# Identity transposes placed in TensorE's program order during the first batch of a two-layer decoder kernel

## What is computed

```python
x = _layernorm(x + _L0_attn_ref(x, ...))      # layer norm, 256->1024 projection, 4-tap convolution, selective scan over 16 states, gate, 512->256
x = _layernorm(x + _L0_xattn_ref(x, ctx_768, ...))   # cosine similarity of projected x and projected context
x = _layernorm(x + _L0_ffn_ref(x, ...))       # 4 low-rank experts, best 2, 256->1024->256
x = _layernorm(x + _L1_attn_ref(x, ...))      # 16 query heads, 4 key heads, rotary positions, low-rank additions to the weights
x = _layernorm(x + _L1_xattn_ref(x, ctx_768, ...))   # single-head attention over the context
x = _layernorm(x + _L1_ffn_ref(x, ...))       # gated recurrence over the 8 batches, c = f*c + i*g, then tanh(x wo + c_final uo + bo)
```

## Time and profile before

| | us |
|---|---|
| median of 3 executions | 1187.26 (1186.92 to 1191.86) |
| the profiled execution, its own time | 1190.96 |
| its span, first to last instruction | 1189.1 |
| TensorE busy (PE in the rows) | 1077.9, 91% of the span |
| VectorE busy (DVE) | 1007.3, 85% |
| ScalarE busy (ACT) | 763.1, 64% |
| GpSimd busy (POOL) | 210.1, 18% |
| mean granted TensorE clock, share of full speed | 0.945 |

### The profile page before, as it was taken

The page is one execution under the profiler, slowest core; times in us unless marked ns, Lnnn a source line. Parts: engine busy times, 40 slices in busy tenths (PEclk is TensorE's granted clock), DMA queues, the critical chain, the costliest instruction groups (busy, mean ns, idle before and its releaser), DMA issues. The chain is left out here.

```text
span 1189.1 us, 17415 instructions
## 1 busy us (share of the span) xinstructions
PE 1077.9 (91%) x6154; PEld 794.7 (67%) x6154; DVE 1007.3 (85%) x1690; ACT 763.1 (64%) x2010; POOL 210.1 (18%) x257
## 2 busy tenths in 40 slices
PE   5574869999999999999999999999999999999984
PEld 3353556665778677776786688767875877677763
DVE  3989899999999999999999999999999994334316
ACT  4525335677767876788667876877677656637533
POOL 0200010021221313130313141313211211010002
PEclk8666859999999999999999999999999999999997
DMA  5421211122333333342434143423342321000302
GB/s 220 152 101 50 71 43 36 46 63 64 84 76 103 72 82 71 63 112 59 94 63 114 28 115 71 119 38 72 89 122 37 79 54 32 1 1 10 128 13 71
DMA packets 41193, 86.70 MB, mean 73 GB/s; under 512 B 3737, under 2 KB 14970, under 8 KB 40466
## 3 DMA queue, kind: packets, MB, share of 16 engines
q1 hardware_dynamic: 27282, 60.42, 15.8%
q0 software_dynamic: 13824, 25.17, 12.2%
HBM read 54.38 MB, written 6.04 MB: 51 GB/s over the span
## 5 line engine op out<-in xcount | busy, mean ns | idle before, releaser
L561 ACT ACTIVATE scans<-dt,a_neg 128x255 f32<-128x255 f32 x512 | 224.1, 499 | 0.1
L632 POOL DMA_DIRECT2D scans<-scans x96 | 84.6, 882 | 422.1 <-DVE scans L606 421.7
L606 DVE TENSOR_TENSOR scans<-scans,BC 128x1024 f32<-128x1024 f32 x128 | 155.7, 1216 | 0.1
L598 DVE TENSOR_TENSOR_SCAN scans<-scans 128x1024 f32<-128x1024 f32 x64 | 146.0, 2281 | 2.7 <-ACT scans L561 2.7
L598 DVE TENSOR_TENSOR_SCAN scans<-scans,dBx_odd 128x1024 f32<-128x1024 f32 x64 | 146.0, 2282 | 2.6 <-ACT scans L561 1.8
L1392 ACT ACTIVATE ya<-bank,nmax 128x256 f32<-128x256 f32 x240 | 111.0, 474 | 41.2 <-issue 28.6
L532 PE MATMUL bank<-ident,scans 128*128 128x128 f32 x640 | 104.3, 302 | 31.2 <-DVE scans L606 30.9
L532 PEld LDWEIGHTS bank<-ident,scans 128*128 128x128 f32 x640 | 84.7, 156 | 53.8 <-DVE scans L606 34.4
L1459 DVE TENSOR_REDUCE nmax<-bank 128x2 f32<-128x512 f32 x128 | 84.6, 682 | 30.6 <-PE bank L1306 30.2
L558 ACT ACTIVATE scans<-neghalf 128x4 f32<-128x4 f32 x128 | 26.7, 208 | 90.1 <-PE bank L532 90.0
L1401 ACT ACTIVATE ya<-bank 128x512 f32<-128x512 f32 x120 | 68.6, 601 | 24.4 <-PE bank L1315 18.8
(11 more groups left out here) (273 smaller groups left out, 2327.3 us busy)
## 6 DMA issues: line engine op xcount, KB each, us to landing
BC<-xpj_scratch SPq DMA_DIRECT2D x31, 1024.0 KB, 5.8
scans<-scans POOLq DMA_DIRECT2D x96, 256.0 KB, 3.3
xin<-in_x SPq DMA_DIRECT2D x8, 256.0 KB, 3.0
conv<-in_x SPq DMA_DIRECT2D x8, 256.0 KB, 3.0
out<-scans SPq DMA_DIRECT2D x8, 256.0 KB, 2.1
kept_x<-x SPq DMA_DIRECT2D x7, 256.0 KB, 3.1
kept_w<-wa SPq DMA_DIRECT2D x7, 256.0 KB, 2.0
BC<-kept_w SPq DMA_DIRECT2D x1, 1792.0 KB, 9.2
```

What stands on the lines that cost most here:

```text
L561: ins = act.activation(step[:, j, 1:S], dt[b % 2][:, c, 1:S], ACT.Exp, scale=a_neg[:, c, n:n + 1])
L598: dve.tensor_tensor_scan(H, H, flat(dBx[u % 2]), 0.0, ALU.mult, ALU.add).then_inc(s["a_scan"], 1)
L606: dve.tensor_tensor(H, H, Ch, ALU.mult).then_inc(s["a_hC"], 1)
L632: pool.dma_start(flat(H[:, 0:2, :]), flat(H[:, 2:4, :]), accum_op=ALU.add).then_inc(SUM_OF[(NU * b + u) % 3], 16)
```

## The change

A new stage K for TensorE, and 87 letters K put into TensorE's list. A piece of K is four transposes of the 128x128 identity, into the four quarters of bank 7. It waits for nothing and signals nothing. Nothing reads what it writes. No letter of the old list moves, and the lists of the other engines stay as they are. 4 times 87 is 348 new matmul instructions and as many weight loads.

```diff
+N_IDLE = 87
...
 ORDER = {
     "pe": (
-        "FFFFFFFFFFSFSSSSSFFYWSFWYSSSFFSYSSFSSFYSSYWFSYGGGWGSSSFWWWYWSWYWYSSYWYSWSFWYFFWSWWWWWWSWWWWYWWFWWYFWWWWWSWWWWY"
...
+        "FFFFFFFFFFSKKFSSKKKKSKKKKKKKKSKKKKSKKFKKKKKKFYWSFWYSSKKKKKKKSKKKKKFFSYKKKSKKKKKKKKKKKKKSFSKKKKSKKKKFYSKKKSYWFS"
+        "YGGGWGKKKKSSSFKKWWWYKKWSWYWKKKKKYSSYKKWYSWKKKKKKKSFWYFFWSWWWWWWSWWWWYWWFWWYFWWWWWSWWWWYFYSFYSYYYYWYYYYFSYYYSYY"
...
+        def idle_pe(pe):
+            for _ in range(N_IDLE):
+                for t in range(4):
+                    pe.transpose(y2[:, t * P:(t + 1) * P], ident[:, :], ident[:, :])
+                yield
...
-                        "V": all_batches(lambda b: v_pe(pe, b))}, ORDER["pe"])
+                        "V": all_batches(lambda b: v_pe(pe, b)),
+                        "K": idle_pe(pe)}, ORDER["pe"])
```

More of the change, by code:

```diff
@@ L47 @@
     "pe": (
-        "FFFFFFFFFFSFSSSSSFFYWSFWYSSSFFSYSSFSSFYSSYWFSYGGGWGSSSFWWWYWSWYWYSSYWYSWSFWYFFWSWWWWWWSWWWWYWWFWWYFWWWWWSWWWWY"
-        "FYSFYSYYYYWYYYYFSYYYSYYFYYSYYYSSVVGGGYYGYFVVSFYYFWWWYWWSWVSYVYSYVVFWFYWYYWSYVYVWFSWWWYWVVWYSYWFWWYWWVSVWWFWWSW"
-        "WWWWYWWYWWVVVSSVVVVVVVYFWYYSWWYWYYWWYSWWYYWYYSYSWYYWSYWWYWWWWWWWYYSWYWWSVVGYWGYGGYVVSYYSSWYWVVWWSYYWYWWFVVFYYV"
-        "FVYSWWWYFYFYVWVWWWWYYWWSYWSWYFWWVVWWFSWWYWWWWWWWSWWVVVVVVVVVSVYSFWYYWWYWYYWWYSWWYYWYSWYYSWYSWYWYWWWYWWSWWYWSYW"
@@ L52 @@
[L52 to L56, removed]
@@ L57 @@
-        "VVSVWVYWWYSYYYWYYYWWYSWWYYWSYWYWYYWSWYWWWWWWWWYSYWWSYVGGWGGVYYWYWWWVVYYWYWWVVYYYVVWYYWYVVWYYWVYVWWWWYYWWVYVWWY"
-        "YWWVVWWVVWWVWWWWWWWWWVVVVVYWYYYYYYYYYYWWYYWYYWYWYWYWYVVYWYYWVVYYWWYWVYYWWWWYVYWYWYVVYYYWWWWYVVWVVYYYVVYVVVVVVV"
-        "WVVVWWWWWWWWWWWWWWWWWWWWWWWWWWWWWWW"
+        "FFFFFFFFFFSKKFSSKKKKSKKKKKKKKSKKKKSKKFKKKKKKFYWSFWYSSKKKKKKKSKKKKKFFSYKKKSKKKKKKKKKKKKKSFSKKKKSKKKKFYSKKKSYWFS"
+        "YGGGWGKKKKSSSFKKWWWYKKWSWYWKKKKKYSSYKKWYSWKKKKKKKSFWYFFWSWWWWWWSWWWWYWWFWWYFWWWWWSWWWWYFYSFYSYYYYWYYYYFSYYYSYY"
@@ new lines @@
+        "FYYSYYYSSVVGGGYYGYFVVSFYYFWWWYWWSWVSYVYSYVVFWFYWYYWSYVYVWFSWWWYWVVWYSYWFWWYWWVSVWWFWWSWWWWWYWWYWWVVVSSVVVVVVVY"
+        "FWYYSWWYWYYWWYSWWYYWYYSYSWYYWSYWWYWWWWWWWYYSWYWWSVVGYWGYGGYVVSYYSSWYWVVWWSYYWYWWFVVFYYVFVYSWWWYFYFYVWVWWWWYYWW"
+        "SYWSWYFWWVVWWFSWWYWWWWWWWSWWVVVVVVVVVSVYSFWYYWWYWYYWWYSWWYYWYSWYYSWYSWYWYWWWYWWSWWYWSYWVYFSVWWGYYGGYGVVSYYSSSV"
+        "YWVWWYYWYWWVFWVYSYFFYVVYWSYWYFFVVWWYYWWWYVWWVFWSYYWWFVVWWVSVWWVWWVWSWWWWWWWVWSVVVFSYWYYSWWYWYYYWWSYWYWYYWYWSSY"
+        "WWYWYWWWYSWWWWWSYYWVYSWWVGYGYGGYVVSSYSWFYWSWWYVVWYYWYVWVYSYYSVVFWYYWYFFWVVWYYSWWWWFWFWVYVWWYSYWWVVWWSVFWWVFWVW"
@@ new lines @@
+        "WWSWWWWWVVVVSVYFYWSYWWYWYYWWYSWWYYYSWYWYYSWWYWYWWYWSWWWWWYSYWSWWGYVGGVGYYSSSFWYVVWWYWYYSWWVWYVYSYVVFFFWYYWYVVS"
+        "YWYSVYWFFWWWWVYWWYSWWVYVWWFWYWYSVVVWWVWWWFWSWWWWWSVVVVVVSYFWYYYWYWYSYWYWWYYWWYSWYWYSYWWWYWWSWWWYWWSWWSYWGWYGGG"
+        "YSSWSFWVVWYWSYWYWWVVYYSYVVWWYWYSVYWVWWYWSWYWWYVVWSWYYWWYWWYVVWSYWWYWWWWVVYYWSWWWVVVVVSVVVSVWVYWWYSYYYWYYYWWYSW"
+        "WYYWSYWYWYYWSWYWWWWWWWWYSYWWSYVGGWGGVYYWYWWWVVYYWYWWVVYYYVVWYYWYVVWYYWVYVWWWWYYWWVYVWWYYWWVVWWVVWWVWWWWWWWWWVV"
+        "VVVYWYYYYYYYYYYWWYYWYYWYWYWYWYVVYWYYWVVYYWWYWVYYWWWWYVYWYWYVVYYYWWWWYVVWVVYYYVVYVVVVVVVWVVVWWWWWWWWWWWWWWWWWWW"
@@ L60 @@
+        "WWWWWWWWWWWW"
     ),
```

## The result

The changed kernel takes 1181.9 us (median of 7 executions, 1180.9 to 1184.1), the kernel before 1188.59 us (median of 7, 1186.92 to 1191.86). The ratio is 0.9936, with a 95% interval of 0.9923 to 0.995: faster by 0.64%, some 6.7 us by the medians. The forecast was 1174.8 us, so the direction was right and the size, 12.5 us, was nearly double the truth. The profiled execution took 1180.91 us, its span is 1179.1 us.

The account below looks back on a forecast made before the run. VectorE was taken to bound the kernel from 35 to 180 us, waiting 14.5 us on a TensorE slowed by its clock. Seven wait terms sum to 12.5 us, taken from the 1187.26 us median: 1174.8 us, range 1169 to 1186.

Parts of the forecast that it names:

- The bound: From 35 to 180 us VectorE bounds; its 14.5 us of waits for TensorE are the most to gain, handed on unchanged.
- The pieces at no cost: The 87 pieces, at most 47 us at full clock, fit TensorE's 51.3 us of idle time and cost nothing.
- Transposes as activity: Float32 transposes against the identity count as activity and raise TensorE's clock, against the Trainium skill's rule.
- L1583: VectorE's 3.2 us wait: the projection and low-rank product ahead shrink to half, 2.0 us gained.
- The two waits at L448: VectorE's waits of 2.6 and 0.8 us: combined weight and projections ahead shrink, 2.1 and 0.8 us gained.
- L1612: VectorE's 1.4 us wait: half of the 2.07 + 1.87 us ahead exceeds it, so all is gained.
- L613: VectorE's 3.7 us wait: work ahead shrinks by 2.7 us, 4.1 with earlier gains, so all is gained.
- L865: VectorE's 2.2 us wait: L532 and the logits shrink by 1.7 us, work ahead by about 1; all gained.
- L913: VectorE's 0.6 us wait: chain already at full clock, TensorE somewhat earlier; half taken, 0.3 us gained.
- I take the clock to stay at 1.00 from the second block on: TensorE's clock, mean 0.68 from 35 to 180 us, would be near 1.00; the 12.5 us sum assumes it.
- the first rival: Half the gain: waits grow as work shrinks, the clock falls again in one or two; 1181 us, chance 0.18.
- The rival on the other side: Slower: pieces run at 1.2 GHz and overrun their waits by 25 to 35 us; +13 us, 1200 us, chance 0.10.

Follow-up runs that it names:

- f3: The changed kernel with twice the pieces in each block (174 in place of 87); 1188.9 us, ratio 0.9985 to the kernel before.
- e2: The changed kernel with each piece two plain 128-row identity products in place of four transposes; 1183.0 us, ratio 0.9935 to the kernel before.
- e1: The changed kernel with each piece two one-row products in place of four transposes; 1204.5 us, ratio 1.0109 to the kernel before.
- e3: The changed kernel with 33 more pieces (120) where TensorE still idled; 1175.9 us, ratio 0.9888 to the kernel before.
- f1: The changed kernel with 33 more pieces where TensorE idled, 22 at the start and 2 more (144); 1173.8 us, ratio 0.9857 to the kernel before.
- f4: The changed kernel with only its first six blocks (26 pieces, up to 60 us); 1186.4 us, ratio 0.9975 to the kernel before.

## Why the prediction was right in direction and double in size

- **The bound** held. VectorE's idle time in the first batch was what could be won, and what was won there arrived at the end. (The digits of rows 1 go down to 5, not to 6; nothing rests on it.)
- **The pieces at no cost** held, with one small exception. The 7 pieces ahead of unit 6 of batch 1 ran mostly at half clock (6.05 us from 164.35), and L534 behind them started at 170.24, 1.6 us after VectorE's product was there (168.64). Behind it L913's wait became 0.1 us longer. f3 shows what it costs when the cover is gone.
- **Transposes as activity** held: the clock rose from 0.68 to 0.91 with them, and e2 shows products of the same size doing no more.
- **The terms, one by one.** L1583: 2.0 forecast, 3.2 to 1.4 is 1.8 measured. The two waits at L448: 2.9 forecast, 3.4 to 0.4 is 3.0. These stand ahead of the first fall of the clock. L1612: 1.4 forecast, 0.9 measured. L613: 3.7 forecast, 1.0 measured. L865: 2.2 forecast, 0.6 measured. L913: 0.3 forecast, 0.1 lost. The sum is 7.2 against 12.5.
- **The step that failed** is "I take the clock to stay at 1.00 from the second block on". It fell at 88, at 115, near 150 and at 160 us. The falls at 115 and 160 us stand directly in front of the work for L1612, L613 and L865, and these three terms miss 4.8 of the 5.3 us. I had named the first rival, with 0.18, and priced it at 1181; the result is 1181.9, while the case that I gave 0.62, 9 to 17 us of gain, did not come. That the price fits so well is partly luck. "Half of 12.5" was not worked out from rows, and the path was another: I wrote that the block behind a fall would run at half clock and overrun, but, except for the one block above, what ran at 1.2 GHz and cost the time was the kernel's own work behind the waits. The falls were also four, not "one or two". I should have seen the step in my own numbers: I checked the blocks against the waits of the kernel before, although the same sum made the work in front of them shorter, by 0.9 us for a unit's transposes alone. The waits at 88 and 115 us grew from 1.8 to 3.5 us.
- **The rest of the difference** of 7.1 us to the forecast: 5.3 us from those terms, 0.7 us from the two small losses at the beginning, which belong to the profiled execution and not to the change, and 1.3 us because the median of the kernel before over seven executions is 1188.59 and not 1187.26. These make 7.3; the 0.2 too many lie within the scatter.
- **The rival on the other side** was real, though not for this kernel: e1 makes it happen, 13.8 us above the kernel before beside it, where I had worked out 13.

## What to carry to other kernels

When the engine with the work in hand is slow only because it comes out of waits at 1.2 GHz, filling the waits with work that nobody needs can pay, provided the work is of a kind that brings the clock up (here 128 rows did and one row did not), is in a bank that nobody reads, and ends before the wait does. Size the blocks against the waits of the kernel that already has the higher clock, not of the one before, and so repeat the step once; here resized blocks brought 0.48% on top of 0.64% (e3), and with the start included 0.79% (f1). Look at the place where a wait feeds the bounding engine without a buffer: it is there that the lateness of all blocks ahead arrives nearly in full.

## What the runs showed that was not expected

An engine that is busy without a break can be held at 1.2 GHz: in e1 all of 30.7 us were occupied, 18.5 us of them by products with one row, at a clock of 0.50, while the same places filled with transposes or products of 128 rows were at 1.00 there. The last 7 us of the stretch, from 69.68 us, had no piece in them: the kernel's own projection, low-rank product and combined weight ran at 1.2 GHz directly behind the one-row pieces.

That may bear on the kernel's own work too. At its end f1 mixes products with one row (L967, the bias) into an otherwise full TensorE:

```profile
1129.43 1.12 PE L967 MATMUL bank<-b_ho,ones 1*128 1x256 f32 x4
...
1135.79 7.45 PE L990 MATMUL bank<-xT,w_g 128*128 128x256 f32 x24 [0.69 <-ACT xT L1146]
1143.17 0.69 PE L967 MATMUL bank<-b_ho,ones 1*128 1x256 f32 x2
```

```profile
1133.10:1139.90 6.80, 6.11 (x16) 4.19 (x15) 0.00 (x0) 1.00 (x3) 0.00 (x0) 0.50 0.01 2
```

The clock was at 1.00 up to 1133.1 us and at 0.50 from there to 1139.9, after work without a gap since 1127.5, and the gates of the recurrence (L990) took 7.45 us. In the profiled execution of the kernel before they took 5.45:

```profile
1148.23 1.13 PE L959 MATMUL bank<-b_ho,ones 1*128 1x256 f32 x4
...
1153.65 5.45 PE L982 MATMUL bank<-xT,w_g 128*128 128x256 f32 x24 [0.69 <-ACT xT L1138]
1159.02 0.69 PE L959 MATMUL bank<-b_ho,ones 1*128 1x256 f32 x2
```

f1's lead over the kernel before is 18.8 us at the first of these steps (1129.43 against 1148.23) and 15.8 us at the last (1143.17 against 1159.02), which is also the difference of the spans. So this one fall cost f1 3.0 us. In f4's profiled execution the clock fell at the same step (1144.3 us); in those of the kernel before, of the change and of e3 it did not, so the same work can run at either clock.

In e3 the clock likewise fell at 116.6 us, within work without a gap since 113.5 us, of which the last are a product of 8 rows and one into a single column. f1 has the same steps at 1.00. Whether the few rows do it in these two places was not tried.
